# Feed-forward part kept with the 2048 units on the partitions: transposes of that tensor removed, int8 products, maxima over tiles

## The chip, the cores and the metric

One Trainium2 chip, one core of it. The metric is the device time of one execution in microseconds (us), median of the executions shown.

## The reference

For 4 batches of 1024 tokens the block adds gated cross-attention and then a gated feed-forward part to `x`. The change touches the second alone:

```
x = x + tanh(g_xattn) * xattn(ctx, layernorm(x), mask, ...)
x = x + tanh(g_ffn)   * ffn(layernorm(x), w1, conv_w, conv_b, w2)

def ffn(x, w1, conv_w, conv_b, w2):     # x (4,1024,512), w1 (2048,512), w2 (512,2048)
    h = bit_linear(x, w1)               # (4,1024,2048)
    h = depthwise_conv1d(h)             # 3 taps along the tokens, for each of 2048 units
    h = silu(h)
    return bit_linear(h, w2)

def bit_linear(x, w):   # act_quant: 127 / max|x| over the token's features, round, back
    return act_quant(x) @ weight_quant(w).T      # weight_quant: -1, 0, 1 times a scale
```

Each token needs the largest magnitude over its 2048 hidden units before any of them can be rounded to integers for the second product.

## The kernel before

The program runs in stages. Queries, keys and values come first, then attention (`c_pe`, `c_act`, `c_dve`), and from 1412.7 us on the feed-forward part. Each engine has its own instruction list in program order. [...] POOL is the GpSimd engine, DVE the vector engine, ACT the scalar engine, PE the tensor engine.

For a batch of 1024 tokens the feed-forward part has two phases. In the first, the 2048 hidden units go by in 16 groups of 128 (index j):

- PE multiplies `w1q` by `xiT` (8 matmuls, line 1419) into one of two pairs of PSUM banks. The units are on the partitions, the 1024 tokens along the free axis.
- DVE multiplies the pair by `row`, the scale of each token, into the SBUF tile `gp` (line 1158). This frees the banks at once.
- ACT makes the middle tap with its bias and the last tap (lines 800, 804), POOL adds the two (672), and DVE adds the first tap (1179).
- PE turns the result with 8 transposes (1448), so that tokens are on the partitions. ACT applies Silu from PSUM into `hT` (823), and DVE takes the maximum over the group's 128 units, which lie side by side (1163).

In the second phase the scales follow from the maxima (1186 to 1193). DVE scales `hT` and adds a constant that rounds (1170), ACT subtracts it into bf16 `hi8` (815), PE turns it back (1434), and ACT copies it out as `hq` (840). PE then multiplies by `w2q` (1461, 16 matmuls for 128 tokens), and DVE scales and adds the residual `x2` (1207). The normalisation of the next batch (862 to 910) lies on DVE in the second phase, between those instructions. The batches run in a hardware loop, the last one apart.

Of the kernel before, what the change touches and what calls it, by code (L numbers as in the profile page):

```python
# [42 lines left out]
def flamingo_gated_block(nc, x, ctxT, mask, mask_cols, g_x, g_f, wsT, bk_cols, b_v, wtT, bq_cols, woT, b_out,  # L43
# [11 lines left out]
    with ExitStack() as ctx:  # L55
# [314 lines left out]
        LN_ACT, LN_ACT_N = counts(["std", "row"] + [f"xT{i}" for i in range(NT // 2)])  # L370
        D_DVE, D_DVE_N = counts(["g0", "g1"]
                                + [f"{w}{j + 2 * (w == 'g') - 2 * (w == 'hmax')}" for j in range(KH) for w in ("g", "c0", "hmax")
                                   if not (w == "g" and j + 2 >= KH) and not (w == "hmax" and j < 2)]
                                + [f"hmax{KH - 2}", f"hmax{KH - 1}", "hm", "hmc", "hrec", "hsc", "hdq"]
# [1151 lines left out]
```

## Time and profile before

| | |
|---|---|
| median of 3 runs | 1929.59 us (1925.8 to 1929.66) |
| the profiled execution's own time | 1929.86 us |
| its span, first to last instruction | 1928.0 us |
| mean granted clock of TensorE | 0.944 of 2.4 GHz |
| PE busy | 1684.4 us (87%) |
| DVE busy | 1216.9 us (63%) |
| ACT busy | 780.3 us (40%) |
| POOL busy | 729.0 us (38%) |

The shares are averages over stages with different limits. In the stage that the change touches they are not the same as in the whole. The profiled execution took 1.9 us more than its span.

### The profile page before, as it was taken

What the parts mean: (1) busy time and instruction counts of PE and PEld (TensorE: products, weight loads), DVE (VectorE), ACT (ScalarE), POOL (GpSimd) and SP (SyncE); (2) the same over time, 40 slices, a digit from 0 to 9 for tenths busy, and PEclk for the clock granted to TensorE, in tenths of its full rate; (3) what the DMA queues carried; (4) which work ended last, traced back from release to release, by engine and by line L of the source; (5) the groups of instructions that cost most, each with busy time, mean ns of one, the idle gap of its engine ahead of it and who ended that gap; (6) DMA issues with size and microseconds to landing.
All of it is one profiled execution on the core that took longest, in us unless ns stands there. A gap on an engine that the chain in (4) does not pass through costs nothing.

```text
span 1928.0 us, 24398 instructions
## 1 busy us (share of the span) xinstructions
PE 1684.4 (87%) x8738; PEld 1038.8 (54%) x8738; DVE 1216.9 (63%) x2270; ACT 780.3 (40%) x793; POOL 729.0 (38%) x317
## 2 busy tenths in 40 slices
PE   6887899999997699999999999999856785967867
PEld 5666678888885344455445444544433443534434
DVE  6777645343433567755765676465269979799793
ACT  2111122222210044433442344245318766787676
POOL 1121000000000088866885688578606134062340
PEclk9989999999998599999999999999979798997988
DMA  6656547444444511114111412041130030120201
GB/s 233 229 181 206 179 170 243 154 149 152 171 145 152 180 56 56 56 66 143 56 57 66 143 57 100 12 143 35 44 131 1 1 131 0 38 92 0 88 1 44
DMA packets 104676, 200.59 MB, mean 104 GB/s; under 512 B 7568, under 2 KB 27024, under 8 KB 104592
## 3 DMA queue, kind: packets, MB, share of 16 engines
q1 hardware_dynamic: 104592, 199.49, 29.5%
q8 instruction: 50, 0.82, 0.2%
q14 instruction: 34, 0.28, 0.0%
HBM read 127.90 MB, written 71.57 MB: 103 GB/s over the span
## 4 chain that ended last, share of the span: by engine, by line
PE 62%; issue 19%; POOL 7%; DVE 6%; DMA 5%; SPq 1%; ACT 1%; POOLq 0%; DVEq 0%; ACTq 0%
PE ps L1260 13%; PE ps L1272 12%; PE ps L1224 9%; PE ps L1226 9%; PE ps L1225 9%; PE ps L1244 6%; DMA wraw<-in_w2T 5%; POOL h_first L672 4%; POOL h_third L672 2%; PE ps L1285 2%; DVE junk L926 1%; PE ps L1461 1%; DVE h_first L1179 1%; POOL acc L667 1%; DVE gp L1158 1%
## 5 line engine op out<-in xcount | busy, mean ns | idle before, releaser
L667 POOL TENSOR_TENSOR acc<-acc,pr 128x1024 f32<-128x1024 f32 x192 | 457.7, 2384 | 118.7 <-ACT pr L684 99.6
L684 ACT ACTIVATE pr<-ps,mcol 128x1024 f32<-128x1024 f32 x256 | 284.3, 1114 | 405.1 <-PE ps L1260 402.3
L926 DVE CUSTOM_DVE_ANT_0 junk<-ps,mbias 128x512 bf16<-128x512 f32 x512 | 333.4, 689 | 171.8 <-PE ps L1244 168.0
L1272 PE MATMUL ps<-pr,vv 128*64 128x512 f32 x1024 | 273.3, 616 | 0.0
L672 POOL TENSOR_TENSOR h_first<-h_first,last_tap 128x1024 f32<-128x1024 f32 x44 | 104.8, 2385 | 306.2 <-ACT last_tap L804 306.2
L650 POOL MEMSET nmt<- 128x128 f32 x1 | 0.2, 204 | 449.1 <-DMA w_ternary<-wtb 449.1
L1244 PE MATMUL ps<-kh,qh 64*128 64x512 f32 x512 | 136.8, 475 | 26.3 <-DVE nmv L926 17.6
L1244 PEld LDWEIGHTS ps<-kh,qh 64*128 64x128 f32 x512 | 57.5, 193 | 148.3 <-issue 101.7
L1419 PE MATMUL ps<-xiT,w1q 128*128 128x512 bf16 x512 | 125.1, 393 | 5.9 <-ACT xiT L790 5.9
L1461 PE MATMUL ps<-w2q,hq 128*128 128x512 bf16 x512 | 120.8, 390 | 2.5 <-ACT hq L840 1.8
L667 POOL TENSOR_TENSOR acc<-pr 128x1024 f32<-128x1024 f32 x32 | 76.8, 2399 | 110.8 <-ACT pr L684 110.8
L1260 PE MATMUL ps<-qh,kh 64*128 64x512 f32 x512 | 116.2, 445 | 0.0
L1448 PE MATMUL ps<-ident,h_first 128*128 128x128 f32 x352 | 57.8, 317 | 66.2 <-DVE h_first L1179 51.8
L1260 PE MATMUL ps<-qh,kl 64*128 64x512 f32 x512 | 102.5, 392 | 0.0
L1260 PE MATMUL ps<-maug,aug 64*128 64x512 f32 x512 | 102.3, 391 | 0.0
L1260 PE MATMUL ps<-ql,kh 64*128 64x512 f32 x512 | 102.0, 390 | 0.0
L1224 PE MATMUL ps<-chh,wsh 128*128 128x512 f32 x256 | 99.7, 389 | 1.7 <-DVE chl L1091 1.7
L1224 PE MATMUL ps<-wsh,chh 128*128 128x512 f32 x256 | 99.7, 389 | 0.3 <-DVE cst L1133 0.3
L1226 PE MATMUL ps<-wsh,chl 128*128 128x512 f32 x256 | 99.6, 389 | 0.0
L1225 PE MATMUL ps<-wsl,chh 128*128 128x512 f32 x256 | 99.6, 389 | 0.0
L1225 PE MATMUL ps<-chl,wsh 128*128 128x512 f32 x256 | 99.6, 389 | 0.0
L1226 PE MATMUL ps<-chh,wsl 128*128 128x512 f32 x256 | 99.6, 389 | 0.0
(152 smaller groups left out, 3179.7 us busy)
## 6 DMA issues: line engine op xcount, KB each, us to landing
craw<-in_ctxT SPq DMA_DIRECT2D x8, 2048.0 KB, 9.7
xa<-in_x SPq DMA_DIRECT2D x8, 1024.0 KB, 6.4
wraw<-in_w1T SPq DMA_DIRECT2D x16, 512.0 KB, 7.3
wraw<-in_w2T SPq DMA_DIRECT2D x16, 512.0 KB, 7.6
q_split<-kqh SPq DMA_DIRECT2D x32, 256.0 KB, 2.0
q_split<-kql SPq DMA_DIRECT2D x32, 256.0 KB, 2.3
base<-lna SPq DMA_DIRECT2D x8, 1024.0 KB, 9.1
k_split<-kqh SPq DMA_DIRECT2D x32, 256.0 KB, 2.2
```

The costliest lines, as they stand in the source:

```text
L667: nc.gpsimd.tensor_tensor(acc[:, blk % 2, :], first, pr[:, (8 * blk + j) % NP, :], ALU.add).then_inc(pool_acc, 1)
L672: nc.gpsimd.tensor_tensor(h[j % 3], h[j % 3], last_tap[j % 2][:], ALU.add).then_inc(pool_tap, 1)
L684: act.activation(pr[:, u % NP, :], ps[:, 2 * (u % 2):2 * (u % 2) + 2, :].rearrange("p a t -> p (a t)"), ACT.Exp, bias=mcol[:, (u // 64) * ...
L926: dve.tensor_tensor_reduce(out=junk[:, e, :], in0=ps[:, 4 + e, :], in1=mbias[:, b % 2, kk * CH:(kk + 1) * CH], scale=-1.0, scalar=3.0e38, ...
L1224: pe.matmul(acc, lh, rh, start=k == 0, stop=False)
L1225: pe.matmul(acc, lh, rl, start=False, stop=False)
L1226: last = pe.matmul(acc, ll, rh, start=False, stop=k == n - 1)
L1244: last = pe.matmul(ps[:, 4 + e, :], qh[g % 3][64 * e:64 * e + 64, i * P:(i + 1) * P], kh[g % 3][64 * e:64 * e + 64, kk * CH:(kk + 1) * CH] ...
L1260: last = pe.matmul(ps[:, 2 * (u % 2) + e, :], of_keys[64 * e:64 * e + 64, :], of_tokens[64 * e:64 * e + 64, :], start=w == 0, stop=w == 3)
L1272: last = pe.matmul(ps[64 * e:64 * e + 64, 6 + blk % 2, :], vv[:, g % 2, j, 64 * e:64 * e + 64], pr[:, u % NP, e * CH:(e + 1) * CH], start= ...
L1419: last = pe.matmul(ps[:, 2 * (j % 2) + t, :], w1q[:, k, j * P:(j + 1) * P], xiT[:, k, t * 512:(t + 1) * 512], start=k == 0, stop=k == KD - 1)
L1461: last = pe.matmul(ps[:, i % 2, :], hq[:, i % 2, j, :], w2q[:, j, :], start=j == 0, stop=j == KH - 1)
```

## The change

The part up to the first matmul of the feed-forward stage is the same. In it:

- The hidden tensor stays with the units on the partitions, as `hh` (18 slots of 1024 tokens). The fp32 transposes of line 1448, the bf16 transposes of line 1434 and ACT's copies of them out of PSUM go.
- `gp` goes. DVE multiplies by `row` inside the PSUM banks. Both taps of ACT and DVE's first tap read those banks, and the pair is free for the next group only when the first tap is done.
- Silu runs on ACT from SBUF to SBUF, in place.
- The maximum over 2048 units is now one over 16 slots and then over partitions. `tensor_reduce` with absolute values reads `hh` as "p j t -> p t j", so that for each token the slots lie 4096 bytes apart: four instructions over 8 slots x 256 tokens during groups 10 to 13, two over 6 slots x 512 tokens and two over 4 slots x 512 tokens behind group 15. Then there are 8 fp32 transposes on PE, a maximum over 128 partitions' values (read from PSUM), and the scale is spread back over partitions by 8 fp32 matmuls with `ident`.
- DVE multiplies each slot by that scale and writes int8 `q8`, and ACT widens it to bf16 `hq`. There is one pass each for all 16 slots.
- The second product of a batch runs during the first phase of the next batch, 8 matmuls between the groups. For the last batch it follows behind.
- The normalisation of the next batch moves into the first phase. Its two scalings run on POOL, the rounding to bf16 on ACT, and statistics and maxima stay on DVE.
- Loops over batches are written out. Loads and stores of `x2` go by 128 tokens.

```diff
-                dve.tensor_tensor(gp[:, j % 3, 1:S + 1], ps[:, 2 * (j % 2):2 * (j % 2) + 2, :].rearrange("p a t -> p (a t)"),
-                                  row[:], ALU.mult).then_inc(dve_d, 1)
+            def scaled(b, j):
+                n, banks = KH * b + j, ps[:, pair(j):pair(j) + 2, :].rearrange("p a t -> p (a t)")
+                dve.wait_ge(pe_h, n + 1)
+                dve.tensor_tensor(banks, banks, row[:], ALU.mult).then_inc(dve_g, 1)
+
+            def first_tap(b, j):
+                n, banks = KH * b + j, ps[:, pair(j):pair(j) + 2, :].rearrange("p a t -> p (a t)")
+                dve.wait_ge(act_tap, 2 * n + 2)
+                dve.scalar_tensor_tensor(out=hh[:, SLOT_OF[j], 1:S], in0=banks[:, 0:S - 1], scalar=convw[:, j, 0:1], in1=hh[:, SLOT_OF[j], 1:S],
+                                         op0=ALU.mult, op1=ALU.add).then_inc(dve_c0, 1)
...
-                dve.tensor_reduce(hmax[:, j, :], hT[:, :, j * P:(j + 1) * P], AX.X, ALU.max, apply_absolute_value=True).then_inc(dve_d, 1)
+                dve.tensor_reduce(out, hh[:, slots, cols].rearrange("p j t -> p t j"), AX.X, ALU.max, apply_absolute_value=True).then_inc(dve_mx, 1)
+
+            def highest_first(b, q):
+                cols = slice(q * 256, (q + 1) * 256)
+                highest(b, slice(0, 8), cols, hh[:, TOP + 1, cols], 8, 0)
+
+            def highest_rest(b):
+                for t in range(2):
+                    cols = slice(t * CH, (t + 1) * CH)
+                    highest(b, slice(TOP + 1, TOP + 7), cols, hh[:, TOP, cols], 13, 4)
+                for t in range(2):
+                    cols = slice(t * CH, (t + 1) * CH)
+                    highest(b, slice(TOP - 3, TOP + 1), cols, tap[:, 0, cols], KH, 5 + t)
...
+                dve.tensor_tensor(q8[:, j % 4, :], hh[:, SLOT_OF[j], :], ps[:, 6:8, :].rearrange("p a t -> p (a t)"), ALU.mult).then_inc(dve_q, 1)
...
+            def spread(cols, bank):
+                for i in range(NT):
+                    last = pe.matmul(ps[:, bank + i // 4, i % 4 * P:(i % 4 + 1) * P], cols[:, i:i + 1].broadcast_to([P, P]), ident[:],
+                                     start=True, stop=True)
+                return last
...
+            def hidden(b, j):
+                n = KH * b + j
+                if j >= 2:
+                    pe.wait_ge(dve_c0, n - 1)
...
+                for j in range(KH):
-                    if j + 3 < KH:
-                        first(j + 3)
+                    if b:
+                        product(NT * (b - 1) + j // 2, j % 2)
+                    if j + 2 < KH:
+                        hidden(b, j + 2)
...
+            def normal(b, i):
+                if i == 0:
+                    pool.wait_ge(dve_rs, b + 1)
+                nc.gpsimd.tensor_scalar(xn[:, i, :], xn[:, i, :], mv2[:, i, 0:1], rs2[:, 1, i:i + 1], ALU.subtract, ALU.mult).then_inc(pool_nm, 1)
...
+            def silu(b, j):
+                act.wait_ge(pool_tap, KH * b + j + 1)
+                act.activation(hh[:, SLOT_OF[j], :], hh[:, SLOT_OF[j], :], ACT.Silu).then_inc(act_silu, 1)
+
+            def widen(b, j):
+                act.wait_ge(dve_q, KH * b + j + 1)
+                if b and j == 0:
+                    act.wait_ge(pe_o, NT * b)
+                act.activation(hq[:, j, :], q8[:, j % 4, :], ACT.Copy).then_inc(act_hq, 1)
```

The instruction lists show what stands between two groups. PE in the kernel before, in the first phase (`w1q` is the first product, `ident` the transposes; the register rows only work out a semaphore's value):

```order
L1416 REGISTER_ALU
L1419 MATMUL ps<-xiT,w1q 128x512 [waits dve_d]
L1419 MATMUL ps<-xiT,w1q 128x512 x7
L1444 REGISTER_ALU
L1446 REGISTER_ALU [waits dve_d]
L1448 MATMUL ps<-ident,h_first 128x128 [waits act_d]
L1448 MATMUL ps<-ident,h_first 128x128 x7
```

PE in the changed kernel, in the first phase of batches 1 to 3 (`w2q` is the second product of the batch before):

```order
L1428 MATMUL ps<-w2q,hq 128x512 x8
L1417 MATMUL ps<-xiT,w1q 128x512 [waits dve_c0]
L1417 MATMUL ps<-xiT,w1q 128x512 x7
L1428 MATMUL ps<-w2q,hq 128x512 [waits act_hq]
L1428 MATMUL ps<-w2q,hq 128x512 x7
```

The transposes between the groups are gone, the second product has taken their place, and a group of the first product now waits for `dve_c0`, which is the first tap two groups back. In batch 0 the `w2q` rows are absent.

DVE in the kernel before, in the first phase:

```order
L1158 TENSOR_TENSOR gp<-ps,row 128x1024
L1179 SCALAR_TENSOR_TENSOR h_third<-gp,convw,h_third 128x1024
L1162 REGISTER_ALU
L1163 TENSOR_REDUCE hmax<-hT 128x8
L1155 REGISTER_ALU
```

DVE in the changed kernel, in groups 13 to 15 of batch 0 and behind them:

```order
L1120 TENSOR_TENSOR ps<-ps,row 128x1024 [waits pe_h]
L1125 SCALAR_TENSOR_TENSOR hh<-ps,convw,hh 128x1023 [waits act_tap]
L1132 TENSOR_REDUCE hh<-hh 128x256 [waits act_silu]
L1120 TENSOR_TENSOR ps<-ps,row 128x1024 [waits pe_h]
L1125 SCALAR_TENSOR_TENSOR hh<-ps,convw,hh 128x1023 [waits act_tap] x2
L1132 TENSOR_REDUCE hh<-hh 128x512 [waits dve_mx,act_silu] x2
L1132 TENSOR_REDUCE tap<-hh 128x512 [waits dve_mx,act_silu] x2
```

The maximum of every group has become a maximum over slots in groups 10 to 13, and four more stand behind the last group, ahead of all that needs a scale.

## Rows read from the trace of the kernel before

**Rows 1.** Busy time by stage: PE, PEld, DVE, ACT, POOL, granted clock, DMA share, GB/s.

```profile
1412.70:1441.50 28.80, 9.47 (x45) 5.24 (x46) 22.66 (x62) 5.20 (x6) 0.00 (x0) 0.59 0.53 187
1441.50:1514.10 72.60, 47.37 (x248) 27.51 (x246) 67.90 (x48) 53.70 (x49) 38.68 (x16) 0.90 0.04 13
...
1562.90:1684.70 121.80, 90.99 (x549) 52.51 (x548) 106.57 (x124) 89.37 (x74) 38.69 (x16) 0.90 0.14 52
...
1805.70:1928.00 122.30, 84.98 (x504) 48.74 (x502) 84.74 (x70) 83.05 (x67) 38.65 (x16) 0.88 0.12 44
```

**Rows 2.** Timeline of one group, batch 0: start us, length us, engine, line, [idle before].

```profile
1479.64 2.37 POOL L672 TENSOR_TENSOR h_first<-h_first,last_tap 128x1024 f32<-128x1024 f32 x1 [1.47 <-ACT last_tap L804]
...
1480.30 1.21 DVE L1158 TENSOR_TENSOR gp<-ps,row 128x1024 f32<-128x1024 f32 x1
1480.31 1.89 PE L1419 MATMUL ps<-xiT,w1q 128*128 128x512 bf16 x8
...
1481.43 1.65 DVE L1179 SCALAR_TENSOR_TENSOR h_third<-gp,convw,h_third 128x1024 f32<-128x1024 f32 x1
...
1483.01 1.21 DVE L1163 TENSOR_REDUCE hmax<-hT 128x8 f32<-128x1024 f32 x1
...
1484.14 1.21 DVE L1158 TENSOR_TENSOR gp<-ps,row 128x1024 f32<-128x1024 f32 x1
```

**Rows 3.** The chain of waits, start of batch 3, at 1.2 GHz: start us, length us.

```profile
1817.06 3.43 PE ps L1419 x8
1820.51 1.23 DVE gp L1158
```

**Rows 4.** Groups of instructions by shape: busy us, mean ns, idle before.

```profile
L1163 DVE TENSOR_REDUCE hmax<-hT 128x8 f32<-128x1024 f32 x64 | 76.9, 1207 | 3.7 <-ACT hT L823 3.7
L891 DVE TENSOR_REDUCE amax<-xn 128x1 f32<-128x512 f32 x32 | 19.6, 683 | 0.0
L933 DVE TENSOR_REDUCE nmt<-nmv 128x16 f32<-128x32 f32 x16 | 3.0, 187 | 2.0 <-issue 0.9
L1186 DVE TENSOR_REDUCE hm<-hmax 128x8 f32<-128x128 f32 x4 | 1.5, 380 | 0.1
L1207 DVE SCALAR_TENSOR_TENSOR x2t<-ps,hdq,x2t 128x512 f32<-128x512 f32 x32 | 23.9, 748 | 40.8 <-PE ps L1461 40.8
L823 ACT ACTIVATE hT<-ps 128x1024 f32<-128x1024 f32 x64 | 65.5, 1024 | 65.4 <-PE ps L1448 64.8
L804 ACT ACTIVATE last_tap<-gp,convw 128x1024 f32<-128x1024 f32 x64 | 72.6, 1134 | 0.0
L639 POOL CAST wsh<-wstage 128x1024 fp32r<-128x1024 f32 x8 | 10.2, 1270 | 105.1 <-DMA wstage<-in_wsT 105.1
L672 POOL TENSOR_TENSOR h_first<-h_first,last_tap 128x1024 f32<-128x1024 f32 x44 | 104.8, 2385 | 306.2 <-ACT last_tap L804 306.2
```

**Rows 5.** Short windows, same columns as rows 1: what PE did at either clock.

```profile
650.00:660.00 10.00, 5.32 (x9) 2.20 (x9) 5.74 (x19) 0.00 (x0) 0.00 (x0) 0.50 0.01 3
1448.00:1452.00 4.00, 1.08 (x9) 1.04 (x10) 3.97 (x2) 2.66 (x3) 4.00 (x2) 0.98 0.00 0
1452.00:1456.00 4.00, 4.00 (x16) 1.87 (x14) 2.62 (x3) 3.19 (x3) 1.75 (x2) 0.59 0.00 0
1476.00:1480.00 4.00, 2.54 (x16) 1.34 (x15) 4.00 (x4) 3.30 (x3) 2.53 (x2) 1.00 0.00 0
```

**Rows 6.** Timeline of PE: fp32 work at 1.2 GHz.

```profile
1429.31 3.78 PE L1233 MATMUL ps<-diag,ones 128*128 128x512 f32 x4 [17.27 <-DVE diag L902]
1815.09 1.97 PE L1448 MATMUL ps<-ident,h_first 128*128 128x128 f32 x8 [4.35 <-DVE h_first L1179]
```

**Rows 7.** Timeline of DVE at the stage's start: batch 0.

```profile
1418.49 0.20 DVE L883 RECIPROCAL rs<-rs 128x8 f32<-128x8 f32 x1 [0.37 <-ACT rs L782]
1441.49 1.23 DVE L1158 TENSOR_TENSOR gp<-ps,row 128x1024 f32<-128x1024 f32 x1 [5.32 <-PE ps L1419]
```

**Rows 8.** The chain's last products, and DMA issues (KB each, us to landing).

```profile
1912.53 6.92 PE ps L1461 x32
q_split<-kqh SPq DMA_DIRECT2D x32, 256.0 KB, 2.0
```

More of the change, by code:

```diff
@@ L370, in flamingo_gated_block @@
[L370 to L374, printed above, removed]
-                                + ["sc0a", "sc0", "sc1", "sc2"] + [f"{w}{i + 3 * (w == 'sc')}" for i in range(NT) for w in ("sc", "o")
-                                                           if not (w == "sc" and i + 3 >= NT)])
@@ L1227, in split_mm @@
             return last
-        def ln_row(pe, b):
-            pe.wait_ge(dve_ln, b * LN_DVE_N + LN_DVE["diag"])
-            for t in range(2):
-                last = pe.matmul(ps[:, 2 + t, :], ones[:], diag[:, 4 * t:4 * t + 4, :], start=True, stop=True)
-            last.then_inc(pe_row, 1)
         def c_pe(pe):
@@ new lines, in scale_row @@
+            def scale_row(b):
+                pe.wait_ge(dve_sc, 4 * b + 4)
+                spread(adq, 2).then_inc(pe_row, 1)
+            def hidden(b, j):
+                n = KH * b + j
+                if j >= 2:
+                    pe.wait_ge(dve_c0, n - 1)
+                elif j == 0 and b:
+                    pe.wait_ge(dve_hm, 5 * b - 4)
+                elif j == 1:
+                    pe.wait_ge(act_row, b + 1)
+                if j == 0:
+                    pe.wait_ge(act_xt, 4 * b + 4)
+                for t in range(2):
+                    for k in range(KD):
+                        last = pe.matmul(ps[:, pair(j) + t, :], w1q[:, k, j * P:(j + 1) * P], xiT[:, k, t * CH:(t + 1) * CH],
+                                         start=k == 0, stop=k == KD - 1)
+                last.then_inc(pe_h, 1)
@@ new lines, in product, with tops_turned @@
+            def product(k, part):
+                i = k % NT
+                if part == 0:
+                    pe.wait_ge(act_hq, KH * (k // NT + 1))
+                    if i >= 2:
+                        pe.wait_ge(dve_o, k - 1)
+                for j in range(8 * part, 8 * part + 8):
+                    last = pe.matmul(ps[:, OUT_BANK[k], :], hq[:, j, i * P:(i + 1) * P], w2q[:, j, :], start=j == 0, stop=j == KH - 1)
+                if part:
+                    last.then_inc(pe_o, 1)
+            def tops_turned(b):
+                pe.wait_ge(dve_mx, 8 * (b + 1))
+                pe.wait_ge(dve_c0, KH * (b + 1))
+                for i in range(NT):
+                    last = pe.transpose(ps[:, i // 4, i % 4 * P:(i % 4 + 1) * P], tap[:, 0, i * P:(i + 1) * P], ident[:])
+                last.then_inc(pe_top, 1)
```

553 lines of the change are left out of this document (251 added, 302 removed).

## Prediction

> **What bounds the kernel now.** I cut the span into stages by busy time first. Up to 1412.7 us nothing changes. The feed-forward stage takes the other 515.3 us: a head of 28.8 us, then batches of about 121.8 us, the last one 122.3 us with its store [rows 1]. In the first phase DVE is the bound (67.9 of 72.6 us busy in batch 0) [rows 1]. The timeline of one group says why: from one `gp` to the next are 3.84 us, all of it `gp` (1.13 us start to start), the first tap (1.58 us here) and `hmax` (1.13 us); PE finishes its 8 matmuls in 1.89 us and waits [rows 2]. DVE never waits for the first product there, because `gp` takes it out of PSUM and the banks are refilled at once.
>
> **The change, step by step.** I write S for the multiplication by `row`, F for DVE's first tap, H for the 8 matmuls of a group.
>
> *The loop over groups.* H of group j+2 waits for F of group j, S of j+2 waits for that H, and in DVE's list S(j+2) stands ahead of F(j+1), as the instruction lists show. So F, H and S follow one another in every group, and nothing overlaps them but what DVE has between F and the next S. S is 1.13 us (start to start, [rows 2]). F reads PSUM and SBUF like the `x2t` instruction: 748 ns for 512 elements, and 511 more at 1.02 ns (the difference of the two plain `tensor_reduce` rows, 524 ns for 512) make 1.27 us [rows 4]. H is 1.89 us at 2.4 GHz [rows 2] and 3.43 us at 1.2 GHz [rows 3], with about 0.2 us for the two hand-overs (0.02 us is the second, [rows 3]; the rest my estimate). A group costs **4.5 us** at 2.4 GHz and **6.0 us** at 1.2 GHz, against 3.8 to 4.3 us now. S writes PSUM, for which no row exists. I take the row with PSUM as input; 0.1 us more would be 6 us over 64 groups. ACT has two taps and Silu, 1.02 to 1.13 us each [rows 4], 3.3 us, and POOL 2.4 us a group. Both hide under 4.5 us.
>
> *What fills the gap.* DVE has 2.1 us minus the hand-over, some 2.0 us, between F and S for other work. Statistics (2 x 0.6 us), maxima of the next batch's input (0.6 us each by the 683 ns row) and the residual (0.67 us) fit, at nothing. Their cover is the wait for H. The maxima over slots don't fit.
>
> *The maxima.* They replace 16 x 1.13 us = 18.1 us in the loop by 4 x 2048 + 2 x 3072 + 2 x 2048 = 18,432 elements. Plain reductions cost 0.15 us plus 1.02 ns an element: 1207 ns for 1024, 683 ns for 512, 187 ns for 32. One row has strided elements, `hm<-hmax`, 32 bytes apart: 380 ns for 128, where the plain line gives 280 [rows 4]. With the same fixed 0.15 us that is 1.8 ns an element. The new reads are 4096 bytes apart, and this row is the only one like them. I take 1.83 ns. The bounds are 1.02 ns (distance doesn't matter) and 2.6 ns (my estimate, as far above the row as plain is below). The Trainium skill (SBUF — State Buffer, "Door 1: The DMA port swizzle") has the same direction: SBUF has lines of 16 bytes, and each access that crosses to a new line pays a penalty. By that rule strided fp32 reads cost more, by the plain rows they don't. The sum by the latter is the rival below. So 2048 elements take 3.9 us, 3072 take 5.8 us.
> In groups 10 to 13 this overruns the gap by 1.9 us each, with the residual in two of them by 2.55 us: 8.9 us in batches 1 to 3, and at 1.2 GHz, where the gap is 3.6 us, next to nothing. Behind group 15: 2 x 5.8 + 2 x 3.9 = 19.3 us. Silu of group 15 is done after some 4 us, so DVE doesn't wait.
>
> *From maxima to integers,* in series: 8 fp32 transposes 1.97 us at 1.2 GHz (PE has stood idle), with hand-over 2.1 [rows 6]; the maximum from PSUM 1.2 and three small instructions at about 0.2 us (by the 187 ns row) 1.9 together [rows 4]; 8 fp32 matmuls of 128 columns, as many columns as the two of 512 that took 3.78 us, 4.0 with hand-over [rows 6]; then 16 multiplications to int8 at 1.13 us, 18.1. ACT's widening (1.13 us, the SBUF row) runs along [rows 4]. After group 15: 19.3 + 2.1 + 1.9 + 4.0 + 18.1 = **45.4 us** to the next batch's first S. The present second phase is 48.8 us (1514.1 to 1562.9), so all that the missing transposes and copies free there comes to 3 us.
>
> *Clock in batch 0.* No second product runs beside it, and PE works 1.9 of 4.5 us. In the first 4 us window where it worked 1.08 us the clock was on its way from 2.4 to 1.2 GHz, at 2.54 of 4 us it held 2.4, and at 1.2 GHz with 5.3 of 10 us busy it stayed at 1.2 [rows 5]. 1.9 of 4.5 us lies nearer the first, and once at 1.2 GHz the loop (3.4 of 6.0 us) is like the last. I take 1.2 GHz for batch 0, and 2.4 GHz for batches 1 to 3, where the second product fills PE to 3.6 of 4.5 us.
>
> *Head.* Statistics end as now, with the reciprocal at 1418.7 us [rows 7]. Then POOL's 8 scalings, unknown: half of the 1270 ns cast is 0.64 us, half of the 2385 ns addition is 1.2 us [rows 4]; I take 0.95, two operations on one tensor. 8 of them to 1426.4, the last maximum and scales to 1427.8, 8 more to 1435.5, the last rounding 1436.2, transposes 1437.1, spread of `adq` 3.6 to 1440.7, H at 1.2 GHz 3.6: first S at **1444.5**, 3 us later than the present 1441.5 [rows 7]. With POOL at 0.64 or 1.2 it is 5 us earlier or 4 later. The Trainium skill (GPSIMD Engine Reference, "Elementwise — side-by-side cycle accounting") has 769 ns for 512 elements of a one-input loop, which would make it 2.9 us earlier; no row here shows it.
>
> *The sum.* Batch 0: S(1) after 3.4 us, 14 groups of 6.0, then S, two taps of ACT and F 4.8: 92.2, and 45.4, is 137.6. Batches 1 and 2: the first S(2) at 8.4 us (the first taps wait for the last widening, PE starts at 1.2 GHz), 13 x 4.5 = 58.5, overruns 8.9, end 4.8: 80.6, residual 0.7, and 45.4, is 126.7 each. Batch 3: 80.6 + 0.7 + 19.3 + 2.1 + 1.9 + 4.0 = 108.6 up to the integers. Then the tail: first slot 2.4 us, 16 slots with 6 matmuls for 6 token tiles each, two at 1.2 GHz (5.1) and 14 at 1.3 (18.2; 0.216 us a matmul, [rows 8]), two token tiles of 16 matmuls 6.9, last residual 0.9, a store of 256 KB 2.3 with its issue [rows 8]: 35.8 us. 1444.5 + 137.6 + 253.4 + 108.6 + 35.8 = 1979.9 us of span, and 1.9 outside it: **1982 us** beside the profiled execution's 1929.9. That execution stands 0.3 us above the median, so I predict **1981 us**, 2.7% slower.
>
> **The rivals.** What a measurement tells from no change here is 0.2%, about 4 us.
> 1. *Distance costs nothing* (1.02 ns). The maxima behind the loop take 11.1 us and not 19.3, those within it overrun by 2.3 and not 8.9: 4 x 8.2 + 3 x 6.6 = 53 us less, **1929 us**, no change. The `hm` row speaks against it; for it, that row is small and is one shape.
> 2. *Faster:* the same reads at the plain rate, with batch 0 at 2.4 GHz. Place: the 18,432 elements a batch. Price: 53 us, and batch 0 is 15 us shorter (92.2 against 77.1): **1914 us**. It decides from about 1.0 ns an element; at 1.83 ns the clock alone can't bring it there. DVE's 1.6 to 2.1 us first taps, slow now beside POOL, are in favour and are already counted in F.
> 3. *Clock holds 2.4 GHz in batch 0,* strided cost as forecast: 15 us less, **1967 us**. For it: 2.54 of 4 us held. Against: 1.9 of 4.5 is well below.
> 4. *Worse:* 2.6 ns an element. 0.8 ns more on 18,432 elements in 4 batches is 57 us, nearly all on the path: up to **2035 us**. POOL at 1.2 us for two scalings beside its addition (4.8 us a group) would add 2 us a batch.
>
> **How the numbers follow.** Forecast 0.45, rival 3 0.16, rival 1 0.13, rival 2 0.13, rival 4 0.13. Faster by over 0.2%: rival 2 and a part of rival 1, 0.19. Within 0.2%: 0.05. Slower: 0.76. The range leaves out most of rival 4 and reaches down to rival 2's edge: 1914 to 2006 us. The forecast's own, from POOL's and S's bounds and the hand-overs, is 1970 to 1995.
>
> **What would show it.** In the new profile: 4.5 us from F to F in batches 1 to 3 with DVE waiting for PE about 2 us in groups without extras; granted clock near 0.5 in batch 0 and 6.0 us a group; 3.9 us for a maximum of 2048 elements and 5.8 for 3072; some 45 us from the last F to the next S; first S near 1444.5. The prediction falls if a reduction over 2048 takes 2.2 us, if S(j+2) runs without waiting for F(j), or if F takes 2 us as the present first tap does beside POOL.

## The result, and the profile after

The changed kernel takes 1992.62 us (median of 4, 1990.76 to 1993.56) against 1928.51 us (median of 4, 1925.8 to 1929.66): a ratio of 1.0333, 95% interval 1.0315 to 1.0351, slower. The forecast was 1981 us. The profiled execution has a span of 1988.9 us.

In what follows S is DVE's multiplication by `row` (line 1120 now), F its first tap (1125), H the 8 matmuls of a group (1417). The code ahead of the feed-forward part is the same in every kernel here, but in the profiled executions it ends anywhere from 1407.5 to 1413.3 us. So stages are compared from DVE's first statistics on. Head: from there to the first S. A batch: from its first S to that of the next, the last one to the end of the span. Group j is the stretch of the loop that holds F of group j. It is measured from the S ahead of that F to the next S.

| us | head | batch 0 | batch 1 | batch 2 | batch 3 | stage |
|---|---|---|---|---|---|---|
| before ([rows 1]) | 28.8 | 121.4 | 121.8 | 121.0 | 122.3 | 515.3 |
| forecast | 31.8 | 137.6 | 126.7 | 126.7 | 144.4 | 567.2 |
| after | 38.0 | 135.6 | 129.8 | 129.7 | 144.7 | 577.8 |

Busy time by stage after the change: us, then PE, PEld, DVE, ACT, POOL, granted clock, DMA share, GB/s. It answers to [rows 1].

```profile
1411.10:1449.10 38.00, 8.87 (x57) 7.24 (x59) 11.79 (x31) 10.12 (x14) 21.86 (x16) 0.55 0.39 138
1449.10:1541.20 92.10, 50.17 (x134) 16.16 (x134) 65.86 (x65) 56.19 (x57) 56.75 (x31) 0.61 0.00 1
1541.20:1584.70 43.50, 12.60 (x71) 9.71 (x72) 37.86 (x27) 22.48 (x24) 2.61 (x2) 0.63 0.14 48
1584.70:1671.10 86.40, 61.28 (x235) 24.00 (x240) 70.71 (x74) 56.30 (x59) 57.50 (x32) 0.89 0.12 39
1671.10:1714.50 43.40, 13.85 (x87) 10.70 (x88) 37.85 (x27) 21.80 (x23) 1.99 (x1) 0.63 0.19 64
```

The first two batches are cut at the last F or just behind it. In its loop DVE is busy 70.7 of 86.4 us in batch 1; it was 67.9 of 72.6 in batch 0 before [rows 1]. So the loop got longer although DVE's list did not become the bound all through it: something makes DVE wait. Behind the loop it is busy 37.9 of 43.5 us, with nothing of the next loop beside it. The timeline shows both. Columns: start us, length us, engine, line, [idle before, releaser].

```profile
1417.18 16.49 POOL L664 TENSOR_SCALAR xn<-xn,mv,rs 128x512 f32<-128x512 f32 x8 [36.46 <-DVE rs L1100]
1435.13 5.38 POOL L670 TENSOR_SCALAR xn<-xn,asc 128x512 f32<-128x512 f32 x8 [1.47 <-DVE asc L1112]
1449.08 1.23 DVE L1120 TENSOR_TENSOR ps<-ps,row 128x1024 f32<-128x1024 f32 x1 [13.91 <-PE ps L1417]
...
1469.05 1.23 DVE L1120 TENSOR_TENSOR ps<-ps,row 128x1024 f32<-128x1024 f32 x1 [2.50 <-PE ps L1417]
1471.52 3.60 PE L1417 MATMUL ps<-xiT,w1q 128*128 128x512 bf16 x8 [2.51 <-DVE hh L1125]
1475.16 1.23 DVE L1120 TENSOR_TENSOR ps<-ps,row 128x1024 f32<-128x1024 f32 x1 [1.96 <-PE ps L1417]
...
1600.49 1.23 DVE L1120 TENSOR_TENSOR ps<-ps,row 128x1024 f32<-128x1024 f32 x1
1601.63 1.27 DVE L1125 SCALAR_TENSOR_TENSOR hh<-ps,convw,hh 128x1023 f32<-128x1023 f32 x1
1602.96 1.90 PE L1417 MATMUL ps<-xiT,w1q 128*128 128x512 bf16 x8 [0.78 <-DVE hh L1125]
1604.90 1.23 DVE L1120 TENSOR_TENSOR ps<-ps,row 128x1024 f32<-128x1024 f32 x1 [0.26 <-PE ps L1417]
...
1625.41 1.22 DVE L1120 TENSOR_TENSOR ps<-ps,row 128x1024 f32<-128x1024 f32 x1
1627.08 4.13 POOL L664 TENSOR_SCALAR xn<-xn,mv,rs 128x512 f32<-128x512 f32 x2
1631.24 0.69 DVE L1104 TENSOR_REDUCE amax<-xn 128x1 f32<-128x512 f32 x1 [1.37 <-POOL xn L664]
1631.84 1.22 DVE L1120 TENSOR_TENSOR ps<-ps,row 128x1024 f32<-128x1024 f32 x1
...
1637.62 2.33 POOL L680 TENSOR_TENSOR hh<-hh,tap 128x1023 f32<-128x1023 f32 x1
1638.40 1.58 DVE L1108 TENSOR_SCALAR amax<-amax 128x8 f32<-128x8 f32 x1
1640.47 1.23 DVE L1120 TENSOR_TENSOR ps<-ps,row 128x1024 f32<-128x1024 f32 x1
...
1671.15 10.72 DVE L1132 TENSOR_REDUCE hh<-hh 128x512 f32<-128x3072 f32 x2
1681.78 7.13 DVE L1132 TENSOR_REDUCE tap<-hh 128x512 f32<-128x2048 f32 x2
...
1972.15 2.07 DVE L1168 SCALAR_TENSOR_TENSOR x2t<-ps,hdq,x2t 128x512 f32<-128x512 f32 x3 [7.06 <-PE ps L1445]
1976.32 0.75 DVE L1168 SCALAR_TENSOR_TENSOR x2t<-ps,hdq,x2t 128x512 f32<-128x512 f32 x1 [2.10 <-DMA x2t<-x]
```

Five things are to be read there. A plain group of batch 1 goes from S to S in 4.41 us (1600.49 to 1604.90), and H starts only after F; at 1.2 GHz in batch 0 H takes 3.60 us and the group 6.11. Where POOL has two scalings, it is POOL that makes the group 6.43 us (1625.41 to 1631.84): its addition, 2.35 us, and 4.13 us of scalings, and DVE's maximum of `xn` waits for them ahead of the next S. The last group of this kind, group 9, takes 8.62 us (to 1640.47): DVE's four small instructions for the scales stand in it as well, and the first of them, on 8 columns, lasts 1.58 us. So groups 6 to 9 of batch 1 take 5.26, 6.43, 6.43 and 8.62 us. Behind the loop stand two maxima of 3072 elements and two of 2048, 17.9 us, which answer to nothing in [rows 2], where each `hmax` of 1.21 us lay in its group. And at the end DVE's residual adds wait for a transfer of `x2t`, 8.4 us in all (the row of line 1168 below). The groups of instructions: busy us, mean ns, idle before. They answer to [rows 4].

```profile
L1120 DVE TENSOR_TENSOR ps<-ps,row 128x1024 f32<-128x1024 f32 x64 | 78.5, 1231 | 62.7 <-PE ps L1417 62.3
L1132 DVE TENSOR_REDUCE hh<-hh 128x256 f32<-128x2048 f32 x16 | 60.0, 3753 | 0.0
L1132 DVE TENSOR_REDUCE hh<-hh 128x512 f32<-128x3072 f32 x8 | 42.8, 5387 | 0.0
L1168 DVE SCALAR_TENSOR_TENSOR x2t<-ps,hdq,x2t 128x512 f32<-128x512 f32 x32 | 23.7, 746 | 15.5 <-DMA x2t<-x 8.4 <-PE ps L1445 7.1
L664 POOL TENSOR_SCALAR xn<-xn,mv,rs 128x512 f32<-128x512 f32 x32 | 66.1, 2075 | 36.5 <-DVE rs L1100 36.5
L670 POOL TENSOR_SCALAR xn<-xn,asc 128x512 f32<-128x512 f32 x32 | 21.8, 700 | 1.5 <-DVE asc L1112 1.5
```

DVE waits 62.7 us ahead of S, nearly all for PE. The kernel before waited 27.6 us at the same place, and only in the first groups of each batch:

```profile
L1158 DVE TENSOR_TENSOR gp<-ps,row 128x1024 f32<-128x1024 f32 x64 | 77.7, 1214 | 27.6 <-PE ps L1419 27.4
```

A scaling with subtraction takes POOL 2075 ns, the other one 700.

### The profile page after: what moved, and what is told of

It is laid out like the page before. It is cut to its first block, busy times and chain, and to the rows that moved or that the text cites. A ratio compares the mean times of both kernels' runs of the same rounds, so it can differ in the third digit from the quotient of the medians.

```text
span 1988.9 us, 21810 instructions
## 1 busy us (share of the span) xinstructions
PE 1631.6 (82%) x7834; PEld 970.2 (49%) x7858; DVE 1224.4 (62%) x2160; ACT 737.6 (37%) x817; POOL 811.4 (41%) x381
## 4 chain that ended last, share of the span: by engine, by line
PE 67%; DVE 17%; issue 5%; DMA 5%; POOL 4%; ACT 1%; SPq 0%; DVEq 0%; ACTq 0%; POOLq 0%
PE ps L1246 13%; PE ps L1258 12%; PE ps L1217 9%; PE ps L1219 9%; PE ps L1218 9%; PE ps L1230 5%; DMA wraw<-in_w2T 4%; DVE hh L1132 3%; PE ps L1417 3%; POOL xn L664 3%; DVE q L1163 3%; DVE hh L1125 2%; DVE ps L1120 2%; PE ps L1271 2%; POOL hh L680 1%
## 5 line engine op out<-in xcount | busy, mean ns | idle before, releaser
L680 POOL TENSOR_TENSOR hh<-hh,tap 128x1023 f32<-128x1023 f32 x64 | 151.0, 2359 | 266.7 <-DVE hh L1125 160.1
L1417 PE MATMUL ps<-xiT,w1q 128*128 128x512 bf16 x503 | 150.4, 453 | 97.1 <-DVE hh L1125 96.4
L1417 PEld LDWEIGHTS ps<-xiT,w1q 128*128 128x128 bf16 x512 | 51.9, 110 | 193.7 <-DVE hh L1125 129.5
L1428 PE MATMUL ps<-w2q,hq 128*128 128x512 bf16 x372 | 97.0, 403 | 43.0 <-ACT hq L827 42.4
L814 ACT ACTIVATE hh<-ps,convb,convw 128x1024 f32<-128x1024 f32 x64 | 77.0, 1203 | 123.1 <-DVE ps L1120 122.8
L1120 DVE TENSOR_TENSOR ps<-ps,row 128x1024 f32<-128x1024 f32 x64 | 78.5, 1231 | 62.7 <-PE ps L1417 62.3
L1132 DVE TENSOR_REDUCE hh<-hh 128x256 f32<-128x2048 f32 (+1 forms) x24 | 102.8, 4298 | 0.0
```

The lines of the kernel that those rows point to most:

```text
L680: nc.gpsimd.tensor_tensor(hh[:, SLOT_OF[j], 0:S - 1], hh[:, SLOT_OF[j], 0:S - 1], tap[:, j % 2, 0:S - 1], ALU.add).then_inc(pool_tap, 1)
L1132: dve.tensor_reduce(out, hh[:, slots, cols].rearrange("p j t -> p t j"), AX.X, ALU.max, apply_absolute_value=True).then_inc(dve_mx, 1)
L1417: last = pe.matmul(ps[:, pair(j) + t, :], w1q[:, k, j * P:(j + 1) * P], xiT[:, k, t * CH:(t + 1) * CH], start=k == 0, stop=k == KD - 1)
```

## The experiments

Each kernel is the changed one with the edit shown, timed beside the kernel before (medians 1926.5 to 1928.7 us). Medians, the ratio to the kernel before with its interval, and the parts of the profiled execution:

| kernel | median us | ratio | head | b0 | b1 | b2 | b3 | stage |
|---|---|---|---|---|---|---|---|---|
| changed | 1992.6 | 1.0333 (1.0315 to 1.0351) | 38.0 | 135.6 | 129.8 | 129.7 | 144.7 | 577.8 |
| e1 plain reads | 1947.8 | 1.0098 (1.0081 to 1.0115) | 37.2 | 124.2 | 118.5 | 119.0 | 133.3 | 532.3 |
| e2 scaling on DVE | 1982.7 | 1.0277 (1.0258 to 1.0295) | 28.6 | 136.4 | 129.8 | 130.9 | 144.0 | 569.7 |
| e3 three pairs | 1961.4 | 1.0165 (1.0148 to 1.0182) | 38.2 | 123.8 | 126.2 | 126.2 | 133.4 | 547.8 |
| e4 PE filled, batch 0 | 1982.6 | 1.0289 (1.0272 to 1.0306) | 38.0 | 128.0 | 130.4 | 129.9 | 144.5 | 570.8 |
| e5 tail buffers | 1982.1 | 1.0288 (1.0271 to 1.0306) | 37.6 | 131.9 | 129.8 | 129.7 | 139.2 | 568.2 |
| e6 running maximum | 1924.9 | 0.9996 (0.9978 to 1.0014) | 37.4 | 126.2 | 114.6 | 114.2 | 126.0 | 518.4 |
| e10 scaling on ACT | 1964.9 | 1.0189 (1.0172 to 1.0206) | 26.8 | 136.2 | 123.1 | 123.0 | 145.2 | 554.2 |
| e14 scaling split | 2013.0 | 1.0443 (1.0425 to 1.0460) | 43.6 | 141.4 | 136.4 | 136.4 | 145.0 | 602.8 |
| e12 = e5, e6, e10 | 1907.7 | 0.9890 (0.9870 to 0.9909) | 27.3 | 126.6 | 109.2 | 109.2 | 121.1 | 493.5 |
| e11 = e12 and e3 | 1863.1 | 0.9663 (0.9647 to 0.9679) | 27.6 | 104.8 | 105.7 | 105.8 | 107.3 | 451.1 |
| e13 = e11 and e4 | 1865.1 | 0.9673 (0.9657 to 0.9689) | 27.7 | 104.9 | 105.8 | 105.8 | 107.3 | 451.5 |

Batch 0 has some noise of its own: in e5, whose edit touches only the last batch, it is 3.7 us shorter than in the changed kernel, with a granted clock of 0.67 in its loop and not 0.61. So a difference of up to 4 us in batch 0 of one execution says nothing. e6, e12, e11 and e13 take the maximum without the absolute value, so they compute slightly less than the others. What the absolute value would cost in that form was not run.

### e1: what does the distance of the reads cost?

```
-dve.tensor_reduce(out, hh[:, slots, cols].rearrange("p j t -> p t j"), ...)
+flat = hh[:, slots, :].rearrange("p j t -> p (j t)")[:, 0:n * k]
+dve.tensor_reduce(out, flat.rearrange("p (t j) -> p t j", j=n), ...)
```

> The maxima read the same number of elements in groups of the same length, but side by side, from fewer slots; the scales are then of the wrong elements. Theory (distance): 2048 elements 2.2 us, 3072 elements 3.3, the eight after the loop 11.1 us and not 17.9; 27 us there and some 17 us in groups 10 to 13 of batches 1 to 3: about 1948 us. Rival (group length): the durations stay at 3.75 and 5.4 us and the time at 1992 us.

```profile
L1134 DVE TENSOR_REDUCE hh<-hh 128x256 f32<-128x2048 f32 x16 | 36.4, 2276 | 0.0
L1134 DVE TENSOR_REDUCE hh<-hh 128x512 f32<-128x3072 f32 x8 | 26.4, 3344 | 0.0
```

The instruction with the same shape goes from 3753 to 2276 ns, and from 5387 to 3344. The stage is 45.5 us shorter, the median 44.8. Of the 45.5 us, 2.7 lie in groups 0 to 9 of batch 0, which the edit doesn't touch. The distance is about seven tenths of the 64.1 us that the change lost. But without it the kernel is still 1.0% slower than before.

### e0: at which distance does the price begin?

Twelve more reductions of 2048 elements, in groups of 8, stand at the end of the program (one run, whose time is not used), twice in the order: side by side, 8, 16, 1024, 4096 and 8192 bytes apart.

```
+probe_reduce(flat[:, 0:4096].rearrange("p (t j s) -> p t j s", j=8, s=2)[:, :, :, 0], 256)    # 8 bytes; s=4: 16 bytes
+probe_reduce(flat[:, 0:8192].rearrange("p (j t) -> p t j", j=8)[:, 0:256], 256)               # 4096 bytes
```

> The changed kernel with 12 more reductions of 2048 elements (groups of 8) at its very end, each twice: side by side, 8, 16 and 1024 bytes apart, 4096 and 8192 bytes apart. Theory (distance): side by side near 2.2 us; from 16 bytes on, where no two elements share a line of 16 bytes, near 3.75 us whatever the distance; 8 bytes apart still near 2.2. Rival (short groups of 8 cost, not distance): all near 3.75 us. Third (banks or far rows): the cost grows with the distance, so that 16 bytes is cheap and 4096 dear. The output is the changed kernel's.

The timeline, one row each, in that order:

```profile
1988.96 2.29 DVE L1219 TENSOR_REDUCE row<-hh 128x256 f32<-128x2048 f32 x1
1991.28 2.29 DVE L1219 TENSOR_REDUCE row<-hh 128x256 f32<-128x2048 f32 x1
1993.60 3.74 DVE L1219 TENSOR_REDUCE row<-hh 128x256 f32<-128x2048 f32 x1
1997.38 3.59 DVE L1219 TENSOR_REDUCE row<-hh 128x256 f32<-128x2048 f32 x1
2001.00 3.59 DVE L1219 TENSOR_REDUCE row<-hh 128x256 f32<-128x2048 f32 x1
2004.63 3.59 DVE L1219 TENSOR_REDUCE row<-hh 128x256 f32<-128x2048 f32 x1
```

8 bytes apart costs nothing, 16 bytes costs at least as much as 8192. The second round gives the same six durations. This is what the Trainium skill (SBUF — State Buffer, "Door 1: The DMA port swizzle") says: lines of 16 bytes, and full rate with two hits in a line. The trace adds the size, 1.3 to 1.45 us on 2048 elements, 0.64 to 0.71 ns an element.

### e6: the maximum without strided reads

```
-    if 10 <= j < 14: highest_first(b, j - 10)          # and highest_rest(b) behind the loop
+    if j >= 3: running(b, j - 3)                        # three more behind the loop
+dve.tensor_tensor(hh[:, TOP, :], hh[:, TOP, :], hh[:, SLOT_OF[j], :], ALU.max)
```

> The maximum over the 2048 units is kept as a running maximum: one tensor_tensor max of two 128x1024 tensors side by side per unit tile, thirteen of them in the loop where VectorE waits for TensorE, two or three behind it; the ten strided reductions are gone. It leaves out the absolute value (the smallest value of Silu is -0.28, so this changes something only for a token whose largest is below that). Theory (strided reads and the work left behind the loop are the cost): behind the loop 17.9 us become 2.5 to 3.5, and groups 10 to 13 fall from 6.0 to 4.5, some 15 + 6 us for each of batches 1 to 3 and 14 for batch 0: 1992 - 75 = 1915 to 1925. Rival (VectorE reading two tensors while GpSimd adds two tensors slows both): each maximum takes 1.6 to 2.2 us, and GpSimd's 2.35 us become 2.8 or more, so that thirteen groups of each batch go from 4.4 to 5.1: 36 us are given back, 1950 to 1960.

```profile
L1134 DVE TENSOR_TENSOR hh<-hh 128x1024 f32<-128x1024 f32 x60 | 83.9, 1399 | 0.9
L680 POOL TENSOR_TENSOR hh<-hh,tap 128x1023 f32<-128x1023 f32 x64 | 179.9, 2813 | 189.8 <-DVE hh L1125 120.7 <-ACT hh L814 69.1
```

The edit takes out eight strided reductions a batch (the expectation says ten). The rival's contention is there: a maximum takes 1399 ns on the mean where it takes 1.22 us undisturbed, and POOL's addition 2813 ns instead of 2359. But it falls into idle time of both, and plain groups stay at 4.41 us. The stage is 59.4 us shorter and the kernel as fast as the one before. The theory's 1915 to 1925 us held, at its upper end. It is worth 14 us more than e1 because the work also left the stretch behind the loop: the strided instructions were costly twice, by distance and by place. From the last F of a batch on, e6 is 3.8 to 6.3 us shorter than e1, 18.7 us in all, and its loops are 4.6 us longer.

### e10, e2 and e14: the scaling that POOL was given

e10 gives the normalisation to ACT, e2 to DVE, e14 leaves it with POOL in two instructions.

```
-nc.gpsimd.tensor_scalar(xn_i, xn_i, mean_i, rstd_i, ALU.subtract, ALU.mult)
+act.activation(xn_i, xn_i, ACT.Identity, bias=minus_mean_rstd_i, scale=rstd_i)      # e10
+dve.tensor_scalar(xn_i, xn_i, mean_i, rstd_i, ALU.subtract, ALU.mult)               # e2
+nc.gpsimd.tensor_scalar(xn_i, xn_i, mean_i, 1.0, ALU.subtract, ALU.mult)            # e14, first
+nc.gpsimd.tensor_scalar(xn_i, xn_i, rstd_i, 0.0, ALU.mult, ALU.add)                 # e14, second
```

> Subtracting the mean and scaling goes back from POOL to DVE, in the same places. Theory (POOL's 2.06 us an instruction is on the path): the head loses 8 us, groups 6 to 9 of batches 1 and 2 fall from 6.4 to about 4.6 us, 7 us each, about 1 us in batch 0: near 1970 us. Rival (DVE waits for GpSimd's access in these instructions, as the 1.58 us small one does): they take 1 to 2 us instead of 0.47 in the loop and the gain is about 10 us, from the head alone.

> The normalisation (subtract the mean, multiply by the inverse deviation, 128x512, eight per batch) goes from GpSimd, where one takes 2.08 us, to ScalarE as one activation with a scale and a bias by row (VectorE prepares the bias, one tiny instruction); its steps in the loop stand one group later. GpSimd keeps the tap's addition and the scaling of 0.70 us. Theory (GpSimd's 2.08 us instead of the 0.95 us foreseen is what lengthens the head and groups 6 to 9): the head falls by 11 to 12 us, groups 6 to 9 of batches 0 to 2 from 6.4 to 4.5 to 4.9 us: 10 to 20 us more, in all 1960 to 1971. Rival (these groups are as long because VectorE's own scans of the tiles and its tiny instruction wait beside GpSimd's addition, as when the normalisation was put on VectorE): only the head's 11 to 12 us, 1980 to 1982.

> GpSimd's normalisation of a 128x512 tile, one instruction with two operands per row (mean and inverse deviation, 2.08 us), is written as two instructions with one operand per row and one constant each, the form that takes 0.70 us in the same kernel; the rest is the changed kernel. Theory (it is the second operand per row that makes it three times as long): two times 0.70 to 0.78 with a wait of 0.1 between, 1.5 us in place of 2.08; head 4 to 5 us shorter, groups 6 to 9 of batches 0 to 2 from 6.43 to 5.3, about 3 us for each of batches 1 and 2: 1980 to 1984. Rival (it is the subtraction, or the tile, not the second operand): the first of the two takes 1.4 us or more, the pair 2.1 or more, and the time is 1992 to 1998.

**e10** has the theory's gain. The head falls by 11.2 us, batches 1 and 2 by 6.7 each. Their groups 6 to 9 are at 4.41 us now, which is 9.1 us less. But the scans of `xn` and the small instructions come one group later and meet a strided maximum there, so that group 10 takes 8.6 us and not 6.6. Batch 0 gives nothing, since at 1.2 GHz its groups take 5.5 to 6.1 us anyway.

**e2** has the head's 9.4 us and nothing in the loop. Its timeline, in a group with two scalings:

```profile
1614.11 1.20 ACT L805 ACTIVATE hh<-ps,convb,convw 128x1024 f32<-128x1024 f32 x1 [3.60 <-DVE ps L1116]
1615.18 3.04 DVE L1096 TENSOR_SCALAR xn<-xn,mv,rs 128x512 f32<-128x512 f32 x2
1615.40 2.53 POOL L673 TENSOR_TENSOR hh<-hh,tap 128x1023 f32<-128x1023 f32 x1 [4.39 <-ACT hh L805]
```

DVE's two scalings take 3.04 us; in the head, without POOL, eight take 3.74. The pair ends 0.3 us after POOL's addition. In the changed kernel the small `amax` instruction (line 1108, 8 columns) does the same: 0.17 us in the head and 1.58 in the loop, where it started at 1638.40, after POOL's addition of 1637.62, and ended with it (1639.98 and 1639.95). That is the rule of the Trainium skill (SBUF — State Buffer, "Who interferes with whom"): DVE instructions that can use two ports for one input, `tensor_scalar` among them, share a pair of ports with GpSimd, and the one that comes first blocks the other for the whole instruction. The trace agrees.

**e14** refuted my theory of two operands per row. One operand with a subtraction is as slow, and multiply with add is fast:

```profile
L665 POOL TENSOR_SCALAR xn<-xn,mv 128x512 f32<-128x512 f32 x32 | 63.9, 1997 | 35.6 <-DVE rs L1103 35.6
L667 POOL TENSOR_SCALAR xn<-xn,rs 128x512 f32<-128x512 f32 x32 | 22.1, 692 | 3.0
```

The pair takes 2.69 us, groups 7 and 8 with two pairs 7.82, and the stage is 25 us longer. It is also the counter-test of e10: more time of POOL in these places lengthens the kernel, by the same path. What about multiplication and addition with two operands per row was not tried.

### e3: a third pair of banks

```
 def pair(j):
-    return 2 * (j % 2)
+    return (0, 2, 6)[j % 3]
 ...
-    if j >= 2: pe.wait_ge(dve_c0, n - 1)                # H(j) waits for F(j - 2)
+    if j >= 3: pe.wait_ge(dve_c0, n - 2)                # for F(j - 3)
```

> A third pair of PSUM banks (6 and 7, idle in the loop) for the first product, so that its matmuls run a group ahead of the first tap. Theory (the chain first tap, matmuls, scaling sets 4.4 us a group and 5.6 to 6.1 in batch 0): plain groups fall to 3.5 to 3.8 us, batch 0 about 20 us shorter and its clock higher, batch 3 about 14, batches 1 and 2 about 8 each (POOL holds four groups at 6.4): near 1943 us. Rival (DVE's own work fills the loop, 70.7 of 86.4 us in batch 1): under 20 us in all.

Banks 6 and 7 also hold the spread scale, so in batches 1 to 3 the third H waits for the last int8 multiplication of the batch before.

The measured 31 us lie between both. DVE's wait ahead of S falls from 62.7 to 20.5 us. The timeline of DVE in batch 3:

```profile
1843.95 1.23 DVE L1120 TENSOR_TENSOR ps<-ps,row 128x1024 f32<-128x1024 f32 x1 [0.38 <-PE ps L1419]
1845.09 1.27 DVE L1125 SCALAR_TENSOR_TENSOR hh<-ps,convw,hh 128x1023 f32<-128x1023 f32 x1
1847.40 1.23 DVE L1120 TENSOR_TENSOR ps<-ps,row 128x1024 f32<-128x1024 f32 x1 [1.04 <-PE ps L1419]
```

A plain group is 3.45 us now, and that is PE itself: 8 matmuls of the first product and 8 of the second at 0.216 us [rows 8]. Batches 0 and 3 win 11.8 and 11.3 us, batches 1 and 2 only 3.6 and 3.5, because there POOL's scalings still hold groups 6 to 9 (7.2, 6.4, 6.4 and 8.6 us) and the strided maxima groups 10 to 13 at 6.0 to 6.6. One cure was hidden behind two other faults.

### e4: the clock of batch 0

```
+else:                                                   # batch 0 has no second product beside it
+    for k in range(8):
+        pe.matmul(ps[:, 5, :], w1q[:, k % KD, 0:P], xiT[:, k % KD, 0:CH], start=k == 0, stop=k == 7)
```

> In batch 0 TensorE has no second product of a batch before, and the granted clock is 0.61 there; a group of eight matmuls takes 3.6 us instead of 1.90, and groups 0 to 5 take 5.5 to 6.1 us instead of 4.4. This kernel adds, in batch 0 alone, eight matmuls per group into a free bank whose result nobody reads; nothing else is changed. If the clock is what lengthens these groups (my theory), groups 0 to 5, 14 and 15 come down to 4.4 to 4.7 us and the time falls by 9 to 14 us, to 1979 to 1984, although TensorE does more work. Rival: the filling (1.7 us at 2.4 GHz, 3.5 at 1.2) only delays the matmuls that VectorE waits for, or the clock stays at 1.2 GHz: then groups stay at 5.5 us or more and the time is 1992 or above.

```profile
1446.20:1481.00 34.80, 28.59 (x128) 11.74 (x126) 25.61 (x35) 27.27 (x26) 19.56 (x9) 1.00 0.01 1
```

With PE busy 28.6 of 34.8 us the granted clock is 1.00, 2.4 GHz, where the changed kernel had 0.63 (18.5 of 32.0 us busy). Groups 1 to 5 fall to 4.41 us. The median falls by 10.0 us, of which the profiled execution shows 7.6 in batch 0; it also entered the stage 2.9 us earlier, which the edit doesn't touch. Useless matmuls made the kernel faster, in the theory's range. Groups 6 to 13 do not gain in sum (50.8 against 49.9 us), because POOL (6.43, and 8.62 in group 9) and the maxima (6.0) hold them.

### e5: the last residual

The last batch's residual gets buffers of its own (`xn`, idle by then) in place of four that are each stored before the next load.

```
-to = x2[:, k % 4, :]
+to = x2[:, k % 4, :] if k < 24 else xn[:, k - 24, :]    # tiles 28 to 31 loaded as soon as the queue is free
```

> The last batch's eight tiles of the residual go through buffers of their own (the idle xn) and are loaded before the end, instead of through four buffers each of which is stored before the next load. Theory: VectorE's last adds waited 8.4 us in all for these loads; without them the stretch from the last batch's first quantised unit to the end falls from 42.0 to 36 to 37 us and the time by 5 to 6 us, to 1987. Rival: the last adds are released by TensorE's last products and the stores behind them, and the loads were hidden: within 1 us of 1992.6.

```profile
L1184 DVE SCALAR_TENSOR_TENSOR xn<-ps,hdq,xn 128x512 f32<-128x512 f32 x8 | 5.5, 744 | 10.3 <-PE ps L1461 7.1 <-DMA xn<-x 2.5 <-PE ps L1467 0.7
```

The waits for the transfer fall from 8.4 to 2.5 us, and batch 3 by 5.5. The median fell by 10.5 us; the rest is 3.7 us in batch 0 and an earlier entry into the stage, neither of which this edit touches. So 5.5 us is what I take for it.

### e12, e11, e13: the repairs together

> Three edits together, each run alone before: the running maximum without absolute values, the normalisation on ScalarE, buffers of their own for the last batch's residual. Theory (three separate costs, which add up: 67.7 + 27.8 + 10.5 = 106 us, and the groups 6 to 9 now free of GpSimd's 6.43 us for both): 1882 to 1892, faster than the kernel before (1928) by about 2%. Rival (with thirteen running maxima beside GpSimd's addition, 1.40 and 2.81 us instead of 1.25 and 2.35, VectorE's statistics and scans no longer fit in the groups, and a part of the gain is lost): 1895 to 1910.

> The same and three pairs of banks for the first product in place of two, which alone gave 31 us. Theory: with the running maximum a group has 1.23 + 1.28 + 1.40 = 3.9 us of VectorE, against the chain of 4.41 that three pairs take away; only 0.4 us per group is left to gain in batches 1 to 3, 5 us per batch, and 1.5 us per group in batch 0, where the chain runs at 1.2 GHz, 15 to 20 us: 25 to 35 us in all, 1855 to 1867. Rival (in batch 0 and elsewhere VectorE with its other steps fills the groups already): within 10 us of the kernel with two pairs.

> The same with the eight filling matmuls per group of batch 0, which hold TensorE's clock there. Theory: with three pairs no wait of VectorE hangs on a group of eight matmuls, so the clock of batch 0 no longer matters: within 3 us of the kernel without them. Rival (the clock is still what batch 0 waits for): 5 to 12 us faster.

**e12** by its stage is 84.3 us shorter than the changed kernel; the three single ones had 59.4 + 23.6 + 5.5 (batch 3 alone) = 88.5. So the costs add up but for 4 us. By medians the sum looked 21 us too large: the single kernels had entered the stage 4 to 6 us earlier than e12 (1413.2 us), and the difference is in code that no edit touched. My 1882 to 1892 us failed, and 1907.7 is in the rival's range. The rival's reason has a small part in it: plain groups are at 4.41 us still, but in batches 1 and 2 the groups with scans or small instructions beside the maximum take 4.6 to 6.3 us, and batch 1 gains 20.6 us where e6 and e10 together had 21.9.

**e11** gained 44.7 us more, above my 25 to 35. Batch 0 gave 21.8. The H of groups 3 to 8 takes 1.90 us and not 3.0 to 3.6, with a granted clock of 0.85 in batch 0's loop and 0.62 in e12. That I had not counted. Why the clock stays up there is not shown; PE does the same 128 matmuls within 72 us in e11 and within 91 in e12. Batch 3 gave 13.8, batches 1 and 2 3.5 each. It is the fastest kernel, 3.4% below the one before. **e13** is within 2 us of it with a clock of 0.95 in batch 0, as expected. The step from 0.85 is small, but it fits that nothing waits for H any more: in two groups H took 2.8 and 3.4 us in e11, and these groups are as long as in e13 (4.64 us), where H runs at 2.4 GHz. A group of e11 in batch 3:

```profile
1779.93 1.23 DVE L1134 TENSOR_TENSOR ps<-ps,row 128x1024 f32<-128x1024 f32 x1
1781.06 1.28 DVE L1139 SCALAR_TENSOR_TENSOR hh<-ps,convw,hh 128x1023 f32<-128x1023 f32 x1
1782.25 1.22 DVE L1148 TENSOR_TENSOR hh<-hh 128x1024 f32<-128x1024 f32 x1
1783.38 0.75 DVE L1176 SCALAR_TENSOR_TENSOR x2t<-ps,hdq,x2t 128x512 f32<-128x512 f32 x1
1784.04 1.23 DVE L1134 TENSOR_TENSOR ps<-ps,row 128x1024 f32<-128x1024 f32 x1
```

DVE has no gap left. It is the bound of the loop again, at 3.45 to 4.12 us a group, with the maximum inside. PE's 16 matmuls of a group, 3.46 us, are close behind it.

## Why the prediction was right, and where its sizes were off

**The loop's chain: right.** F, H and S follow one another. Forecast 4.5 us a group at 2.4 GHz and 6.0 at 1.2; measured 4.41 and 5.5 to 6.1. S took 1.13 us start to start, as forecast from the row with PSUM as input, and F 1.28 (1.27). e3 shows the chain to be the cause by taking it away.

**The clock of batch 0: right.** 0.61 granted, where rival 3 wanted 2.4 GHz. Batch 0 was 2.0 us shorter than forecast, but not by its groups: some took 5.5 us and group 9 took 7.35, so the 14 took 85.8 us against 84.0. The second S came after 1.7 us and not 3.4, and the part from the last S on took 48.1 us and not 50.2. e4 gives the clock's price, 7.6 us less in batch 0 (3.9 against the luckier batch 0 of e5), where rival 3 had 15: groups 6 to 13 were held by others as well.

**Strided maxima: right, slightly too dear.** Forecast 1.83 ns an element, 3.9 and 5.8 us; measured 3.75 and 5.39, behind the loop 17.9 us against 19.3. Rival 1 priced the distance at 53 us, e1 at 45.5. In groups 10 to 13 the forecast's overrun of 1.9 us, with residual 2.55, is measured as 1.6 and 2.2 (6.0 and 6.6 us). From the last F to the next S were 43.3 us in batch 0, forecast 45.4. The 1.83 ns came from a single row at 32 bytes and came out at 1.70 to 1.76. That the same price holds at 4096 bytes was a guess, which e0 bears out.

**POOL's scalings: the step that was mis-sized.** The term was 0.95 us an instruction for both scalings, bounded by 0.64 and 1.2. The one with multiply and add takes 0.70, the one with subtract and multiply 2.08, outside the bounds. The rows of the kernel before held a cast and an addition, and neither has a subtraction with an operand per row. The head came out 6.2 us longer than forecast: the first eight scalings took 16.5 us and the second eight 5.4, where both had 7.6. In the loop POOL has 2.35 + 4.13 us in a group, which rival 4 had at 4.8 in all and I took as hidden: groups 6 to 9 of batches 0 to 2. In batch 1 these four groups stand 9.1 us above the plain 4.41. About 2.1 of them are the four small instructions of group 9, which the forecast left out; the longest waits beside POOL's addition. The rest of the batch was 6.0 us shorter than forecast: the third S came 1.4 us earlier, the plain groups and the maxima in the loop took 2.4 less, the end 2.2 less. So batches 1 and 2 came out only 3 us too long. e10 shows the cause in both places, 11.2 us in the head and 6.7 in a batch.

**The tail: a wait that was not foreseen.** From the first int8 tile to the end I had 35.8 us; it took 42.0. I reckoned with PE's last products and one store. The four buffers of `x2t` must each be stored and loaded again between two adds, and that chain ends last: 8.4 us of waits, of which e5 took away 5.5 us of time.

**The sum.** The errors are +6.2 (head), -2.0 (batch 0), +3.1 and +3.0 (batches 1 and 2) and +0.3 (batch 3, where -5.9 up to the integers and +6.2 behind them cancel): 10.6 us of stage, 577.8 against 567.2. That the errors of batch 3 cancel is luck. The profiled stage began 1.6 us earlier, so 1988.9 us of span against 1979.9. The profiled execution took 1990.8 us, the shortest of four, and the median is 1992.6 against 1981. One sum of the prediction is off: rival 4's 57 us on top of 1981 are 2038 us and not 2035, which changes nothing in the reading.

**Where the gain of the change went.** It frees PE of 16 x 8 fp32 transposes and ACT of their copies, but in the first phase neither was what DVE waited for [rows 1, 2]. It takes `gp` out of the loop, and with it the early release of the banks, and puts the maxima into 18,432 elements at 1.75 ns, over half of them behind the loop. e11 keeps the new layout, without those costs and without POOL's slow scaling and the late transfers, and wins by 65 us over the kernel before: the layout was not at fault. It leaves out the absolute value, so its gain is that of a kernel which does slightly less.

**Open.** Why the unchanged part ahead takes from 1407.5 to 1413.3 us by kernel, whether the subtraction alone makes POOL's scaling slow, and why batch 0's clock differs between executions of the same code (0.61 and 0.67).

## What to carry to other kernels

When a change takes an SBUF copy out between a matmul and its consumers, follow what the copy released: with two pairs of banks the matmuls, the multiplication and the last reader become one chain, and DVE's idle time before them is its price. Put a reduction where the engine waits anyway, in the form of one elementwise maximum per tile over data that lie side by side, not as a few large strided ones behind the loop. And single costs hide one another: the third pair of banks was worth 31 us alone and 44.7 after the other repairs, so try cures together before dropping one.
